# A graph layer with a feed-forward block: the edge sum in wider groups, and the passage into the MLP without drains

## What is computed

```python
aggr = segment_sum(edge_attr_256, dst, 6250)           # 100000 edges x 256, dst is sorted
collected = concatenate([layernorm(x), aggr])          # 6250 x 512
h = relu(collected @ W1 + b1); h = relu(h @ W2 + b2)
x = x + h @ W3 + b3
x = x + slice_attention(layernorm(x))                  # softmax over 64 slices in each of 8 heads
```

## Time and profile before

| | |
|---|---|
| median of three runs | 752.93 us |
| the profiled execution | 754.04 us, its span 752.2 us |
| PE busy | 726.1 us, 97% of the span |
| DVE, ACT, POOL busy | 452.1, 262.5, 244.0 us |
| mean granted TensorE clock | 0.992 |
| moved by DMA | 118.96 MB in 70136 packets |

### The profile page before, as it was taken

One profiled execution on the slowest core, in us unless ns is written; L12 is line 12 of the kernel. 1 busy time (PEld: TensorE's weight loads), 2 busy tenths in 40 slices (PEclk: granted clock), 3 DMA queues, 4 the chain that ended last, 5 costly groups with the idle time before them and its releaser, 6 DMA issues.

```text
span 752.2 us, 13498 instructions
## 1 busy us (share of the span) xinstructions
PE 726.1 (97%) x3865; PEld 472.6 (63%) x3865; DVE 452.1 (60%) x1158; ACT 262.5 (35%) x460; POOL 244.0 (32%) x306
## 2 busy tenths in 40 slices
PE   6999999999999999699999989999999999899997
PEld 3667777677677776365566655555555555588886
DVE  5667666676676666054444378788887887532222
ACT  4344443444444435111221223333333333233331
POOL 3011011010110111213323336565655556244441
PEclk9999999999999999899999999999999999999999
DMA  8999999999999995210000000000000000012222
GB/s 301 375 369 384 384 385 384 384 385 384 385 384 384 385 384 209 71 44 1 0 0 0 0 1 1 0 0 0 0 0 0 0 0 1 0 43 77 76 70 75
DMA packets 70136, 118.96 MB, mean 158 GB/s; under 512 B 4925, under 2 KB 19608, under 8 KB 70120
## 3 DMA queue, kind: packets, MB, share of 16 engines
q1 hardware_dynamic: 69304, 118.50, 43.9%
q10 hardware_dynamic: 816, 0.26, 0.1%
HBM read 112.35 MB, written 6.40 MB: 158 GB/s over the span
## 4 chain that ended last, share of the span: by engine, by line
PE 94%; DMA 2%; DVE 2%; issue 1%; ACT 0%; SPq 0%; DVEq 0%; ACTq 0%
PE ps L1002 23%; PE ps L1239 11%; PE ps L1155 11%; PE ps L1163 11%; PE ps L1047 6%; PE ps L1080 6%; PE ps L1088 6%; PE ps L1098 6%; PE ps L1014 5%; PE ps L1172 3%; PE ps L1039 2%; PE ps L1147 1%; DMA ring_mem<-edge_attr_in 1%; DMA big<-dst_in 1%; PE ps L969 0%
## 5 line engine op out<-in xcount | busy, mean ns | idle before, releaser
L1002 PE MATMUL ps<-ring_mem,side 128*64 128x256 f32 x1564 | 184.1, 385 | 3.7 <-DMA ring_mem<-edge_attr_in 3.5
L719 DVE TENSOR_TENSOR big<-big,ps 128x128 f32 x391 | 112.5, 288 | 73.4 <-issue 31.3
L1002 PEld LDWEIGHTS ps<-ring_mem,side 128*64 128x64 f32 x1564 | 111.4, 137 | 62.5 <-issue 18.4
L558 ACT ACTIVATE side<-ps 128x512 f32<-128x512 f32 x98 | 58.5, 597 | 145.7 <-PE ps L1002 145.3
L1163 PE MATMUL ps<-side,ring_mem 128*128 128x512 f32 x196 | 92.3, 593 | 1.0 <-ACT ring_mem L591 1.0
L1155 PE MATMUL ps<-ring_mem,xn 128*128 128x512 f32 x196 | 92.3, 593 | 0.6 <-DVE ring_mem L877 0.6
L452 POOL TENSOR_TENSOR var_e<-mv,eps 128x2 f32<-128x2 f32 (+1 forms) x25 | 13.1, 522 | 242.9 <-DVE mv L705 242.9
L653 DVE TENSOR_TENSOR side<-iota_w,rel 128x512 f32<-128x512 f32 x98 | 66.3, 678 | 20.6 <-PE ps L1014 20.5
L1239 PE MATMUL ps<-side,ring_mem 128*128 128x256 f32 x360 | 77.9, 379 | 0.0
L506 POOL TENSOR_TENSOR ring_mem<-ring_mem 128x512 f32<-128x512 f32 x49 | 67.0, 1366 | 30.9 <-DVE ring_mem L877 30.9
L1239 PEld LDWEIGHTS ps<-side,ring_mem 128*128 128x128 f32 x360 | 68.4, 190 | 9.3
(11 more groups left out here) (138 smaller groups left out, 889.2 us busy)
## 6 DMA issues: line engine op xcount, KB each, us to landing
ring_mem<-edge_attr_in SPq DMA_DIRECT2D x97, 1024.0 KB, 9.0
x_sb<-x_in SPq DMA_DIRECT2D x24, 256.0 KB, 7.3
result<-ring_mem SPq DMA_DIRECT2D x24, 256.0 KB, 2.1
ring_mem<-edge_attr_in SPq DMA_DIRECT2D x1, 512.0 KB, 6.1
ring_mem<-L_gnn_W_in SPq DMA_DIRECT2D x2, 256.0 KB, 3.4
xn<-L_ffn_W_x_in SPq DMA_DIRECT2D x1, 512.0 KB, 3.5
ring_mem<-L_ffn_W_fx_in SPq DMA_DIRECT2D x1, 512.0 KB, 4.1
ring_mem<-L_ffn_W_out_in SPq DMA_DIRECT2D x1, 512.0 KB, 5.2
```

Source lines behind the costliest of these rows:

```text
L558: act.activation(win_sb[:, s % 2, :], ps[:, SUM_BANKS[s % 2], :], ACT.Copy).then_inc(win_ready, 1)
L719: dve.tensor_tensor(win, win, pair[:, :, (g % 2) * WINDOW:(g % 2 + 1) * WINDOW], ALU.add).then_inc(groups_added, 1)
L1002: last = mm(ps[side_of * WINDOW:(side_of + 1) * WINDOW, SUM_BANKS[s % 2], pair * F:(pair + 1) * F], lhsT=hot[0:parts, s, g * ROWS_PER_PART ...
```

## The change

**Edges.** The first 84 chunks have two groups in place of four. In the first 40 a chunk is one run: each partition holds eight edges that follow each other, a DMA row is 8 KB, and the two "groups" are the first and the second four edges of each partition, with the same base. In chunks 40 to 83 a group is 512 edges, each partition holds four that follow each other, a DMA row is 4 KB. The last 14 chunks stay as they were. PE still does eight products for a chunk, but two transposes, ACT copies half a bank, and DVE adds twice. On the reference's inputs the widest run of 1024 in the first part spans 52 nodes and the widest group of 512 spans 57, so the general pass isn't taken.

```diff
+def run_chunks(eng, step, peel_front, last_trip, total, apart=False):
+    for t in range(peel_front * UNROLL):
+        step(t, t % UNROLL, t // UNROLL, 1 if apart else 2)
+    loops = [(peel_front, WHOLE // UNROLL, 1), (WHOLE // UNROLL, PAIRED // UNROLL, 2)]
+    for lo, hi, groups in loops if apart else [(peel_front, PAIRED // UNROLL, 2)]:
...
+            def chunk_rows(c, groups):
+                rows = edges[bass.ds(c * CHUNK_EDGES, CHUNK_EDGES), :]
+                return rows.rearrange("(g p k) f -> p g (k f)", g=groups, p=P) if groups > 1 else rows.rearrange(
+                    "(p k) f -> p (k f)", p=P)
...
-                sp.dma_start(ring[:, s].rearrange("p g k f -> p g (k f)"),
-                                 edges[bass.ds(c * CHUNK_EDGES, CHUNK_EDGES), :].rearrange(
-                                     "(g p k) f -> p g (k f)", p=P, k=ROWS_PER_PART)).then_inc(edge_in[s], 16)
+                    sp.dma_start(slot(s, groups), chunk_rows(c, groups)).then_inc(edge_in[s], 16)
...
+                cols = groups // 2 * F
-                act.activation(win_sb[:, s % 2, :], ps[:, SUM_BANKS[s % 2], :], ACT.Copy).then_inc(win_ready, 1)
+                act.activation(win_sb[:, s % 2, 0:cols], ps[:, SUM_BANKS[s % 2], 0:cols], ACT.Copy).then_inc(win_ready, 1)
...
-                for pair in range(CHUNK_PAIRS):
+                for pair in range(groups // 2):
                     for h in range(KF):
                         cols = slice(pair * F + h * P, pair * F + (h + 1) * P)
                         last = tr(ps[:, TURN_BANKS[s], cols], win_sb[:, s % 2, cols], ident[:, :])
```

```diff
             sp.dma_start(w1b_sb, w1[F:2 * F, :].rearrange("(k p) n -> p k n", p=P)).then_inc(w1b_in, 16)
-            sp.wait_ge(edges_done, 1)
-            far = sp.value_load(far_i[0:1, 0:1], min_val=0, max_val=1)
...
-            sp.wait_ge(edges_done, 2)
+            for k in range(KF):
+                sp.dma_start(wx[k], w_x[k * P:(k + 1) * P, :]).then_inc(fold_in, 16)
             sp.dma_start(b3_bc, b3.rearrange("(a n) -> a n", a=1).broadcast_to([P, F])).then_inc(b3_in, 16)
-            sp.wait_ge(h1x_ready, 2 * (EDGE_TRIPS + 1))
...
             ln_pair(EDGE_TRIPS, 1)
-            pool.wait_ge(edges_done, 2)
+            pool.wait_ge(win_psum, (FULL_CHUNKS // UNROLL) * UNROLL)
+            pool.memset(blk_s, 0.0).then_inc(blk_clear, 1)
...
+            fold_transposes()
+            pe.wait_ge(groups_added, CREDIT + sums_ahead(CHUNKS - 2, CHUNK_GROUPS))
             ln_transposes(EDGE_TRIPS, 1, bank=7)
-            pe.wait_ge(edges_done, 1)
-            far = pe.value_load(far_i[0:1, 0:1], min_val=0, max_val=1)
...
+            pe.wait_ge(groups_added, CREDIT + ALL_SUMS)
...
-            layer1(0, 4 * P)
+            layer1(0, 4 * P, bank=2)
             for m in range(KF):
                 first_layer_x(EDGE_TRIPS, 1, m, bank=5 + m)
+            pe.wait_ge(wx_ready, KF)
+            layer1(1, 4 * P)
             pe.wait_ge(w23_in, 32)
             layer2(0, 4 * P, l2_banks)
-            layer1(1, 4 * P)
```

More of the change, by code:

```diff
@@ L322, in rest_of_dst @@
                 row = dst.rearrange("(a e) -> a e", a=1)
[L323 to L328, removed]
+                tail = E - FULL_CHUNKS * CHUNK_EDGES
+                sp.dma_start(dst_few[FEW - 1:FEW, 0:tail], row[:, E - tail:E]).then_inc(dst_in, 16)
@@ L329, in chunk @@
+                sp.dma_start(dst_few[FEW - 1:FEW, tail:TAIL_GROUPS * GROUP],
+                             row[:, E - (TAIL_GROUPS * GROUP - tail):E]).then_inc(dst_in, 16)
+            def chunk(c, s, i, groups):
                 if past(c, UNROLL):
@@ L571, in _ @@
             copy_h1x(EDGE_TRIPS - 1, 2, 1, 4)
+            act.wait_ge(fold_t, 1)
+            for k in range(KF):
+                act.activation(wx_t[:, k].rearrange("p j n -> p (j n)"), ps[:, k, :], ACT.Copy).then_inc(wx_ready, 1)
             copy_ln_t(EDGE_TRIPS, 1, 7)
@@ new lines, in base_row @@
+            def base_row(rows, base, bank, col):
+                for g in range(base.shape[1]):
+                    tr(ps[0:1, bank, col + g * rows:col + (g + 1) * rows], base[:, g:g + 1], ident[0:rows, 0:rows])
+            def rest_of_table():
+                pe.wait_ge(prep_v, 15)
+                base_row(PAIRED - WHOLE, base_two, 5, 128)
+                base_row(FEW, base_few, 5, 256)
+                into_columns(PAIRED - WHOLE, 2, rel_two, 4)
+                into_columns(FEW, CHUNK_GROUPS, rel_few, 5).then_inc(prep_t, 1)
@@ L1009, in turn @@
                 pe.wait_ge(win_ready, c + 1)
[L1010 to L1011 removed]
+                behind = sums_ahead(c - 3, groups) if past(c, 3) else -2 * (3 - c)
+                pe.wait_ge(groups_added, behind + CREDIT)
+                for pair in range(groups // 2):
                     for h in range(KF):
@@ L1070, in _, with fold_transposes @@
-            with pe.If(far > 0):
-                with pe.Fori(0, GROUPS - 1) as g:
-                    far_group(g, P)
-                far_group(GROUPS - 1, LAST_PARTS)
-            pe.wait_ge(edges_done, 2)
-            def layer1(i, cols):
+            def fold_transposes():
+                pe.wait_ge(fold_in, 16 * 7)
+                pe.wait_ge(win_ready, CHUNKS)
+                for k in range(KF):
+                    for j in range(PAIRS):
+                        last = tr(ps[:, k, j * P:(j + 1) * P], wx[k][:, j * P:(j + 1) * P], ident[:, :])
+                last.then_inc(fold_t, 1)
@@ L1126, in _ @@
             last.then_inc(fold_t, 1)
-            layer2(2, 4 * P, l2_banks)
-            layer1(3, 4 * P)
-            layer3(2, 4)
-            pe.wait_ge(fold_v, 7)
+            layer3(0, 4)
+            layer2(1, 4 * P, l2_banks)
+            layer1(2, 4 * P)
+            pe.wait_ge(fold_v, 5)
             for j in range(PAIRS):
@@ L1134, in _ @@
             last.then_inc(fold_t, 1)
-            with pe.Fori(3, MLP_CHUNKS - 1) as i:
+            layer3(1, 4)
+            with pe.Fori(2, MLP_CHUNKS - 1) as i:
                 layer2(i, 4 * P, l2_banks)
```

412 lines of the change are left out of this document (236 added, 176 removed).

## The result

The changed kernel takes 737.27 us in the median of 4 runs (737.02 to 737.78). The kernel before took 753.11 us beside it (752.92 to 754.10). The ratio is 0.9784, with an interval of 0.9773 to 0.9796. The forecast was 736.0 in a range of 729 to 746, so it was off by 1.3 us.

What follows compares the result with a forecast made beforehand. The prediction took DMA to bound the edges, with PE 0.1 us a trip behind. Edges -10.0 and passage -1.4, -2.9, -1.7, -0.9 made -16.9 us from the profiled 754.04: 737.1, or 736.0 as median, range 729 to 746.

Steps and rivals of the forecast that it cites:

- rows of 4 and 8 KB: Edges, first 84 chunks: longer DMA rows raise the rate from 384-386 to 401 and 409 GB/s, 10.8 us less.
- start, with the flag's load: Start of the edges: 0.5 us won back from thin-queue stretches, 1.3 us lost to PE's earlier load of the flag.
- start of the MLP: Passage from edges to MLP: drains, register loads and branches go, first product at 303.9 in place of 305.3, -1.4 us.
- clock: Passage: TensorE's granted clock stays up, so the MLP's first product takes 3.43 in place of 6.37 us, -2.9 us.
- gap: Behind the MLP's first product: the second chunk's first layer, put ahead, covers the second layer's 1.68 us wait, -1.7 us.
- fold's transposes: Between two MLP chunks: 0.87 us of transposes leave the path for the wait ahead of the second layer, -0.9 us.
- Which engine binds: Edges: DMA binds at 11.6 us a trip, PE 0.1 us behind; DMA still binds after, so saved transposes alone give nothing.
- Rival 1: Edges: 384 to 385 GB/s is a ceiling whatever the row; only the passage's -6.9 us counts, 746.0 us; chance 0.20.
- the queue covers it: Edges, behind chunk 7: the low end for PE's flag load, 0 us, against 1.3 taken and 2.8 at most.
- a branch, for which I take 0.4: Passage, ahead of the MLP's first product: PE's branch, priced at 0.4 us within the estimate of 303.9 us.
- PE stands still for 2.5 us and then has work: Passage: PE idle from 299.6 to 302.1 us, 2.5 in place of 5.7, then working, so its clock stays up.
- Rival 3: Passage: the clock falls all the same despite only 2.5 us of standstill, about 2.9 us not won, 738.9 us; chance 0.20.

Runs made afterwards that it cites:

- the kernel with fewer products: The changed kernel with a quarter of the window products of the first 84 chunks left out: 738.40 us, ratio 0.9798 to the kernel before.
- the kernel busy in the gap: The changed kernel with three products that nobody reads put in PE's queue ahead of the branch over the general pass: 736.06 us.

## Why the prediction was right, and where it was not

The total was off by 1.3 us. Its terms were off by more, with both signs:

| term | forecast | measured |
|---|---|---|
| rows of 4 and 8 KB | -10.8 | -12.2 |
| start, with the flag's load | +0.8 | -0.9 |
| seam where groups of 256 edges begin | none | +0.65 |
| start of the MLP | -1.4 | -0.4 |
| clock | -2.9 | -1.0 |
| gap | -1.7 | -1.7 |
| fold's transposes | -0.9 | -0.9 |
| sum | -16.9 | -16.4 |

**Which engine binds.** Right, and now shown from both sides: with PE's old work the long rows are worth next to nothing, and with less work for PE the rate stays. The saved transposes were worth nothing by themselves, as said: with 2 KB rows and the transposes saved the edges' trips are 11.6 again.

**The rate.** The mechanism, that a KB costs less in a longer row, is right, and the size too small. Forecast were 401 and 409 GB/s, measured 405 and up to 412; trips of 11.18 and 10.98, measured 10.99 and 10.87. The term that was mis-sized is the 41.2 ns to a KB, taken as the difference of rows of 1 and 2 KB and carried on to longer ones. The record of single packets in the traces gives the rows themselves, as means. In the kernel before (60 to 283 us) they are 48.3 ns for 1 KB and 89.0 for 2 KB, so the two readings of the prediction were right. In the kernel after they are 164.5 ns for 4 KB (130 to 235 us; forecast 171.5) and 322 for 8 KB (40 to 110 us; forecast 336.3), and 317 for 8 KB in the kernel with fewer products. From 1 to 2 KB the KB costs 40.7 ns, from 2 to 4 KB 37.7, and from 4 to 8 KB 38.1 to 39.4: the cost isn't the straight line that the prediction took. The Trainium skill's 3 cycles to a packet (DMA: Bandwidth & Descriptors, "Why small descriptors are slow (HBM only)") would have given half of what was measured, 6 us for 12. From 2 to 4 KB alone, 384 to 405 GB/s, the time for the same bytes is 5.2% less, where its estimate was 2.2%. Rival 1, the ceiling, fell. The 358 GB/s of the Trainium skill's HBM Reference is no limit on this core either; below its table the same section says that a core streaming alone measures well above its share.

**The start.** The flag's load was priced at 1.3 us and cost nothing that shows. It stands here:

```profile
L1128 PEldq TENSOR_LOAD <-far_i x1: 485/485/485, 34.4 to 34.4; - x1
```

It takes 0.49 us, while PE has work in its queue; the turns and the sums of chunk 8 follow without a gap, and the trip it stands in takes 10.68, one of the shortest. So the end "the queue covers it" was met. The price was misread as well: the 1.1 us of the earlier trace rows are DVE's load of the bases, while the flag's load took 0.31 us on DVE and 0.49 on PE in the kernel before. This load stands behind the first mark, so the 0.9 us by which that mark is earlier are not about it. They lie within the scatter of the start (33.01 to 34.83 with the same code), and no run separates the new table from it.

**The seam.** Not foreseen. Groups of 256 edges begin in the trip from 241.72, which takes 11.59 as it should. The trip behind it takes 12.33, and the third 11.52. The row's length isn't the cause: with rows of 2 KB throughout the same second trip takes 12.63 (its neighbours 11.59 and 11.55). With rows of 4 KB it is 11.51, and the next 11.88. It isn't bound to one trip: with fewer products it is the first (12.10), in the kernel busy in the gap the third (12.40). What does cause it stays open.

**The start of the MLP.** The step that failed is "a branch, for which I take 0.4". The loads and the transposes came as laid out: W_slice 8.5 us behind the last group of sums, where 9.7 were expected. The branch took 3.68 us, 2.68 of them uncovered, and leaving it out gave that back. The rows had no price for it. The 2.78 us of "issue" in the earlier trace rows, which the prediction kept as the other end, are DVE's, between its own branch and its second drain. PE's branch took 0.34 us in the kernel before, so 0.4 was right for that kernel and wrong for the changed one, where it took 3.32 to 3.92 in nine kernels. The block it skips has grown, from 104 products in the text to 364, and stands elsewhere. No run changes its length or its place alone, so what made the branch dear is not shown. On DVE the uncovered time stayed as it was (2.61, against 2.78 in the earlier trace rows).

**The clock.** "PE stands still for 2.5 us and then has work" was wrong for the same reason. It stood still for 1.56, worked 1.31, and stood still again for 2.68. The clock was 0.57 for four microseconds and 1.0 us of the 2.9 was won. The kernel busy in the gap showed that the remaining 1.9 are the standstill's. Rival 3, the cold passage, came true for two thirds of its 2.9 us.

**The gap and the fold.** Both to a tenth of a microsecond. Taking the order back brought the wait of 1.68 back.

So that the total came this near is in part luck: the rows gave 1.4 and the start 1.7 more than said, and the passage and the seam 3.6 less. What is left of the 1.3 us is in the step from the profiled execution to the median, for which I took the 1.1 of the kernel before: after, it is 0.1.

## What to carry to other kernels

When two engines stand within 1% of each other, a change pays only if it relieves both: here the longer rows without the saved transposes ended the edges 2.7 us earlier, the saved transposes without the longer rows not at all, and both together 12.5. A branch over a block that isn't run can cost the engine over 3 us even when its condition has long been in a register, and its price in another version of the kernel (0.34 us here) is no guide, so read it again after the change, put it where the engine waits for something else, and ask next what becomes late in its place. A short standstill costs twice, by itself and by the slower clock of the products behind it, and a few products without use inside it take back the second part.

## What was unexpected of the hardware

- In a full queue a DMA row of 1, 2, 4 and 8 KB took 48.3, 89.0, 164.5 and 317 to 322 ns. One core reached 384, 405 and 408 to 412 GB/s with the last three, with no ceiling below, and the rates stayed when PE took less of the time.
- Cutting a load of 1 MB into four DMAs of 256 KB on one queue cost nothing (753.78 us against 753.41, interval of the ratio 0.9991 to 1.001; first mark at 34.78 against 34.77).
- The branch over the skipped block took 0.34 to 0.36 us on PE in the two kernels with the old block and 3.32 to 3.92 in the nine with the new one, although there PE has loaded the flag in its second trip. On DVE the branch itself takes 0.06 us, and 2.58 to 2.84 without work follow; it was not left out there in any run.
- Behind two standstills the first eight products took 5.37 us in three kernels (the second standstill 2.46, 2.56 and 2.68 us) and 5.97, 6.17 and 6.70 in three others (2.80, 2.78 and 2.78). How cold a passage gets can't be read off the standstill to a microsecond, so a term for the clock needs a range of its own.
- The start of a kernel scatters: with the same code for the edges the first mark came at 33.01 to 34.83 us and the last sums began at 278.01 to 280.89.
